# Expert matmuls of a mixture-of-experts layer in row tiles of 64, with destinations in rings of twelve

## What is computed

```python
C = CAP_FACTOR * ((A + E - 1) // E)          # 384 places for an expert
buf = zeros(E, C, D).at[se, pos_c].add(x[st])
g = jnp.einsum('ecd,efd->ecf', buf, w_gate)  # E 64, D 256, F 176
u = jnp.einsum('ecd,efd->ecf', buf, w_up)
eo = jnp.einsum('ecf,edf->ecd', jax.nn.silu(g) * u, w_down)
gathered = eo[se, pos_c] * (sw * valid)[:, None]
y = zeros_like(x).at[st].add(gathered)
```

## Time and profile before

| | before |
|---|---|
| median of 3 runs | 639.82 us |
| lowest, highest | 635.39, 646.47 us |
| span of the profiled execution | 538.8 us |
| TensorE busy, matmuls | 509.7 us, 95% |
| TensorE busy, weight loads | 425.6 us, 79% |
| VectorE, ScalarE, GpSimd busy | 345.0, 299.8, 334.1 us |
| DMA, mean | 221 GB/s |
| mean granted TensorE clock | 0.979 |

### The profile page before, as it was taken

One profiled execution on the slowest core, in us unless ns is written; L12 is line 12 of the kernel. 1 busy time (PEld: TensorE's weight loads), 2 busy tenths in 40 slices (PEclk: granted clock), 3 DMA queues, 4 the chain that ended last, 5 costly groups with the idle time before them and its releaser, 6 DMA issues.

```text
span 538.8 us, 13623 instructions
## 1 busy us (share of the span) xinstructions
PE 509.7 (95%) x4267; PEld 425.6 (79%) x4267; DVE 345.0 (64%) x1107; ACT 299.8 (56%) x899; POOL 334.1 (62%) x365
## 2 busy tenths in 40 slices
PE   8799999999999988998999999999999999999992
PEld 7698999889888877886777887777777877877681
DVE  3976888999999977753555555555554545456412
ACT  4797978999999842120444444545445444544420
POOL 4564254776566668730466776767777767778850
PEclk9898999999999979998999999999999999999997
DMA  8999999752222222269999999999999999967557
GB/s 283 402 375 395 401 400 385 233 212 102 94 92 102 103 75 100 105 211 317 234 256 235 240 235 239 245 241 247 267 236 249 236 241 245 241 110 118 58 121 155
DMA packets 65857, 119.01 MB, mean 221 GB/s; under 512 B 11216, under 2 KB 43280, under 8 KB 62704
## 3 DMA queue, kind: packets, MB, share of 16 engines
q0 software_dynamic: 24576, 56.39, 40.2%
q1 hardware_dynamic: 39584, 58.75, 35.4%
q10 hardware_dynamic: 1616, 2.90, 1.5%
HBM read 57.28 MB, written 60.23 MB: 218 GB/s over the span
## 4 chain that ended last, share of the span: by engine, by line
PE 55%; issue 1%; DMA 1%; DVE 1%; SPq 1%; ACT 0%; DVEq 0%
PE PS L960 18%; PE PS L978 10%; PE PS L964 8%; PE PS L981 7%; PE PS L947 4%; PE PS L811 3%; PE PS L797 2%; PE PS L786 1%; DMA XG<-expert_rows 1%; SPq L483 0%; SPq L470 0%; SPq L469 0%; SPq L468 0%; ACT YE L1236 0%; DVE hot L1410 0%
## 5 line engine op out<-in xcount | busy, mean ns | idle before, releaser
L1838 POOL DMA_INDIRECT expert_rows<-XR,slot x96 | 95.9, 999 | 50.7 <-issue 31.0
L1861 POOL DMA_INDIRECT acc_b<-YE,dest x64 | 93.7, 1465 | 43.9 <-issue 20.5
L1861 POOL DMA_INDIRECT out<-YE,dest x64 | 93.6, 1462 | 34.2 <-issue 13.3
L1236 ACT ACTIVATE YE<-PS,wsel 104x256 f32<-104x256 f32 (+14 forms) x128 | 53.5, 468 | 96.0 <-PE PS L981 96.0
L1063 ACT ACTIVATE SMX<-SMX,smax 128x112 f32<-128x112 f32 x256 | 75.0, 387 | 3.5 <-DVE smax L1466 3.5
L1651 DVE TENSOR_TENSOR HE<-SL,PS 128x216 f32<-128x216 f32 (+12 forms) x64 | 23.2, 362 | 56.1 <-ACT SL L1223 55.4
L1642 DVE COPY XET<-PS 128x432 f32<-128x432 f32 (+12 forms) x64 | 36.6, 572 | 18.8 <-PE PS L947 18.4
L1628 DVE SCALAR_TENSOR_TENSOR hit<-XG,by_rank 112x12 f32<-112x12 f32 (+3 forms) x64 | 14.6, 228 | 41.3 <-DMA acc_b<-YE,dest 21.9
L1223 ACT ACTIVATE SL<-PS 128x216 f32<-128x216 f32 (+12 forms) x64 | 21.6, 337 | 31.6 <-PE PS L960 30.8
L960 PE MATMUL PS<-XET,W 128*128 128x256 f32 (+9 forms) x192 | 38.3, 342 | 0.3 <-issue 0.2
L960 PEld LDWEIGHTS PS<-XET,W 128*128 128x128 f32 x192 | 30.8, 189 | 8.9 <-issue 8.2
(11 more groups left out here) (236 smaller groups left out, 1119.8 us busy)
## 6 DMA issues: line engine op xcount, KB each, us to landing
expert_rows<-zero POOLq DMA_DIRECT2D x24, 1088.0 KB, 13.8
W<-in_w SPq DMA_DIRECT2D x24, 368.0 KB, 3.8
XG<-expert_rows SPq DMA_DIRECT2D x24, 238.0 KB
XB<-in_w SPq DMA_DIRECT2D x15, 368.0 KB, 3.6
SMX<-in_w SPq DMA_DIRECT2D x15, 368.0 KB, 3.5
XG<-expert_rows SPq DMA_DIRECT2D x24, 204.0 KB
W<-in_w SPq DMA_DIRECT2D x24, 128.0 KB, 3.8
XG<-expert_rows SPq DMA_DIRECT2D x10, 272.0 KB
```

Of the source, the lines that this page charges most:

```text
L1236: act.mul(YE[0:h, e.slot, t, :], PS[0:h, 5 + t, e.odd * D:(e.odd + 1) * D], wsel[0:h, e.slot, t:t + 1]).then_inc(y_ready, 1)
L1838: pool.indirect_dma_start(rows, bass.IndirectOffsetOnAxis(ap=slot[:, d2 % UN, k:k + 1], axis=0), XR[:, d2 % UN, :], None, bounds_check=EX ...
L1861: pool.indirect_dma_start(target, bass.IndirectOffsetOnAxis(ap=dest[0:h, e.slot, t:t + 1], axis=0), YE[0:h, e.slot, t, :], None, bounds_ch ...
```

## The change

TensorE's part of the expert stage is written anew (the rare branch keeps the old form in `third_tiles`). Every product is cut into halves of 64 rows of the summed dimension, and a half on rows 0 to 63 is issued beside one on rows 64 to 127 that belongs to another result in another PSUM bank: gate beside up, tail beside gate, token tile beside token tile. Since two halves of one result meet in one bank, TensorE waits for its own earlier half (`h_half`, `d_half`). The down products run one step later, `down(e-1)` in step e, in two pieces. The rows are transposed 64 by 64, into two banks of which there is one pair instead of two, so a transpose waits for the copy of the expert just before. VectorE copies in two instructions, and does copy, choices, product, tail in this order; ScalarE weights `e-1` between the two silus. `dest` and `wsel` are rings of twelve, so `choices` waits for additions twelve experts back. SyncE's text is the same.

```diff
-        wsel = sb("wsel", [P, UN, 2])
+        wsel = sb("wsel", [P, AHEAD, 2])
-        dest = sb("dest", [P, UN, 2], I32)
+        dest = sb("dest", [P, AHEAD, 2], I32)
+        T_ps = PS[:, 0:2, 0:4 * HP].rearrange("p k (d t r) -> p k d t r", d=DC, t=2)
...
+                def waits_rows(e):
+                    hold(pe, xg_loaded[e.slot], e.turn(16, 16))
+                    if not e.first():
+                        hold(pe, et_evac, e.times(1))
+
+                def rows_t(e, t):
+                    for d in range(DC):
+                        for k in range(2):
+                            r = row_half(k)
+                            mm = pe.transpose(T_ps[:, k, d, t, :], XG[r, e.slot, t, d * P:(d + 1) * P], ident[r, r])
+                    return mm
+
+                def product(e, k, o, d, start=False, stop=False):
+
+                    q, n, r = e.odd, 2 * half(e), row_half(k)
+                    into = (PS[:, 2, 0:n], PS[:, UP[q], 0:n], PS[0:W1C - 2 * P, 3, 0:n])[o]
+                    return pe.matmul(into, W1S[home(e)][r, d, o * P:min((o + 1) * P, W1C)], XET[r, q, d, 0:n],
+                                     start=start, stop=stop)
+
+                def hidden_1(e):
+                    pe.wait_ge(ew_loaded[home(e)], e.turn(48, 48, AHEAD))
+                    pe.wait_ge(et_evac, e.times(1, 1))
+                    if not e.first():
+                        pe.wait_ge(silu_ready, e.times(2, -1))
+                    if not e.first(2):
+                        pe.wait_ge(h_ready, e.times(2, -3))
+                    product(e, 0, 1, 0, start=True)
+                    product(e, 1, 0, 0, start=True)
+                    product(e, 0, 1, 1)
+                    product(e, 1, 0, 1).then_inc(h_half, 1)
+
+                def hidden_2(e):
+
+                    pe.wait_ge(h_half, e.times(2, 1))
+                    if not e.first():
+                        pe.wait_ge(h_ready, e.times(2))
+                    product(e, 0, 0, 0)
+                    product(e, 1, 2, 0, start=True)
+                    product(e, 0, 0, 1, stop=True).then_inc(gu_done, 1)
+                    product(e, 1, 2, 1).then_inc(h_half, 1)
+
+                def hidden_3(e):
+
+                    pe.wait_ge(h_half, e.times(2, 2))
+                    product(e, 0, 2, 0)
+                    product(e, 1, 1, 0)
+                    product(e, 0, 2, 1, stop=True)
+                    product(e, 1, 1, 1, stop=True).then_inc(gt_done, 1)
...
+                def down_1(e):
+                    pe.wait_ge(h_ready, e.times(2, 2))
+                    pe.wait_ge(w2_doubled, e.times(1, 1))
+                    if not e.first():
+                        pe.wait_ge(y_ready, e.times(2))
+                    weighing(e, 0, 0, 0, start=True)
+                    weighing(e, 1, 1, 0, start=True)
+                    weighing(e, 0, 0, 1)
+                    weighing(e, 1, 1, 1).then_inc(d_half, 1)
+
+                def down_2(e):
+
+                    pe.wait_ge(d_half, e.times(1, 1))
+                    weighing(e, 0, 1, 0, stop=True)
+                    weighing(e, 1, 0, 0, stop=True).then_inc(dn_done, 1)
+
+                def step(e):
+                    nxt, ahead, last = e + 1, e + 2, e - 1
+                    if has(nxt, EX):
+                        hidden_1(nxt)
+                    if has(ahead, EX):
+                        waits_rows(ahead)
+                        rows_t(ahead, 0)
+                    if has(last, EX):
+                        down_1(last)
+                    if has(ahead, EX):
+                        rows_t(ahead, 1).then_inc(et_done, 1)
+                    if has(nxt, EX):
+                        hidden_2(nxt)
+                    if has(last, EX):
+                        down_2(last)
+                    if has(nxt, EX):
+                        hidden_3(nxt)
...
                 def step(e):
                     if has(e + 1, end):
-                        silus(e + 1)
+                        silu_main(e + 1)
+                    if has(e - 1, end):
+                        weighted(e - 1)
+                    if has(e + 1, end):
+                        silu_tail(e + 1)
+                    if has(e + 2, end):
+                        doubled(e + 2)
...
-                    if not e.first(UN):
+                    if nt == 1:
                         dve.wait_ge(y_stored[j], adds_before(e, nt))
+                    elif not e.first(AHEAD):
+                        dve.wait_ge(y_stored[j], e.turn(32, 32 - 32 * AHEAD // UN))
...
+                    if nt == 2:
+                        to = XET[:, e.odd, :, 0:n].rearrange("p d (t n) -> p d t n", t=2)
+                        dve.tensor_copy(to[:, :, :, 0:HP], T_ps[:, 0])
+                        dve.tensor_copy(to[:, :, :, HP:n // 2], T_ps[:, 1, :, :, 0:n // 2 - HP]).then_inc(et_evac, 1)
+                        return
```

More of the change, by code:

```diff
@@ L32 @@
 P = 128
+HP = P // 2
 T, D = 2048, 256
@@ L316, in build @@
         gu_done, gt_done = sem("gu_done"), sem("gt_done")
+        h_half, d_half = sem("h_half"), sem("d_half")
         silu_ready, h_ready = sem("silu_ready"), sem("h_ready")
@@ L939, in rows_t, with third_tiles @@
+            def third_tiles():
+                pe.wait_ge(et_evac, EX)
+                pe.wait_ge(y_ready, 2 * EX)
                 def rows_t(e):
-                    h = half(e)
                     pe.wait_ge(xg_loaded[e.slot], e.turn(16, 16))
[L943 to L948, removed]
+                    pe.wait_ge(et_evac, e.times(1, -1))
+                    for d in range(DC):
+                        mm = pe.transpose(PS[:, e.odd, d * MAIN:d * MAIN + P], XG[:, e.slot, 0, d * P:(d + 1) * P], ident[:, :])
@@ L968, in down @@
                 def down(e):
-                    j, q, h = home(e), e.odd, half(e)
+                    j, q = home(e), e.odd
                     pe.wait_ge(h_ready, e.times(2, 2))
[L972 to L975, removed]
+                    pe.wait_ge(y_ready, e.times(1, EX))
                     c = slice(q * D, (q + 1) * D)
[L977 to L983, removed]
+                    pe.matmul(PS[:, 5, c], HE[:, q, 0, 0:P], W2S[j][:, 0, :], start=True, stop=False)
+                    pe.matmul(PS[:, 5, c], HE[0:FT, q, 1, 0:P], W2S[j][0:FT, 1, :], start=False, stop=True).then_inc(dn_done, 1)
                 def step(e):
-                    if has(e + 1, end):
+                    if has(e + 1, 2 * EX):
                         hidden(e + 1)
-                    if has(e + 2, end):
+                    if has(e + 2, 2 * EX):
                         rows_t(e + 2)
                     down(e)
[L992 to L1004, removed]
-                in_flight(pe, step, half is even_half)
+                rows_t(Step(EX))
+                rows_t(Step(EX + 1))
+                hidden(Step(EX))
+                rest_in_flight(pe, step)
             def closing():
@@ L1246, in step, with third @@
                     if has(e + 1, end):
-                        silus(e + 1)
+                        silu_main(e + 1)
[5 more added lines that the diff above has]
+                        doubled(e + 2)
+                def third(e):
+                    if has(e + 1, end):
+                        silu_main(e + 1)
+                        silu_tail(e + 1)
                     weighted(e)
-                    if nt == 2 and has(e + 2, end):
-                        doubled(e + 2)
                 if nt == 1:
-                    silus(Step(EX))
-                    rest_in_flight(act, step)
+                    silu_main(Step(EX))
+                    silu_tail(Step(EX))
+                    rest_in_flight(act, third)
                     return
@@ L1257, in experts @@
                 doubled(Step(1))
-                silus(Step(0))
+                silu_main(Step(0))
+                silu_tail(Step(0))
                 in_flight(act, step, half is even_half)
+                step(Step(EX))
             def closing():
@@ L1659, in tail_products, with third @@
                         i = dve.tensor_tensor(HE[64 * t:64 * t + FT, q, 1, c], SL[0:FT, q, 1, c],
-                                              PS[64:64 + FT, TAIL[q], c], ALU.mult)
+                                              PS[64:64 + FT, 3 if nt == 2 else TAIL[q], c], ALU.mult)
                     i.then_inc(h_ready, 1)
                 def step(e):
+                    if has(e + 2, end):
+                        rows_t(e + 2)
+                    if has(e + 1, end):
+                        choices(e + 1)
+                        product(e + 1)
+                        tail_products(e + 1)
+                def third(e):
                     if has(e + 1, end):
@@ L1674, in experts @@
                 rows_t(first + 1)
-                if nt == 2:
-                    pair_add(NPAIR - 2)
-                    pair_add(NPAIR - 1)
+                if nt == 1:
+                    choices(first)
+                    product(first)
+                    tail_products(first)
```

(4 more changed lines are left out.)

76 lines of the change are left out of this document (50 added, 26 removed).

## The result

The changed kernel takes **681.5 us** in the median (677.7 to 691.3, 4 runs) where the kernel before takes 640.6 in the runs beside it: ratio 1.0625, 95% interval 1.057 to 1.068, or +40.8 us. The forecast was 677 us and +37.

The account below looks back on a forecast made before the run. TensorE was taken to bound the expert stage; after the change, late expert rows would. +40.6 for 52 steps, -2 at the start, -1.4 at the end sum to +37: 677 us, +5.8%, range 646 to 703.

Parts of the forecast that it names:

- The loop: Steps 3 to 55: late down products delay expert rows and stall transposes; 4.83 us a step for 4.05, +40.6 us; chance 0.77.
- SyncE's part: In SyncE's queue: from the down products' end, past three weight pieces, to the issue of the rows, 2.97 us.
- The landing: Expert rows, from issue to arrival behind the weights: taken as 4.1 us, range 2.9 to 5.1.
- Hardly depending on the rows: Steps 3 to 55: the stalled step stays about 4.83 us whatever number of rows the experts have.
- Steps 0 to 3 and the end: First steps lack a down product and save 0.4 each: -2 us; one more down and weighting at the end: +1.6.
- Steps 55 to 63: No weights left to fetch, so the loop is open: 3.56 us a step at GpSimd's pace for 3.94, -3.0 us.
- TensorE's own step: Expert stage at halves of 108 rows, nothing late: 3.82 us against 4.25, 0.43 saved.
- the sign of loads that bound: Starts of L962 in one row tile over 0.19 us apart at 216 columns would mean loads bound, not rows.
- a floor: GpSimd's issue of two additions for an expert: 3.46 us a step at small experts, under the 3.73 taken now.
- rows in time: Faster rival: expert rows arrive before their transposes, so no stall; -23 us, 617 us; chance 0.08.
- additions as a bound: Rival: additions bound anyway, so the change does nothing measurable; counted with the within-2% rival, chance 0.10.
- 101 us outside of the span: Median run of 639.8 us is 101 more than the profiled span; that distance was kept for the forecast.

Follow-up runs that it names:

- after_again: The changed kernel unchanged, run again on another chip: 684.11 us, ratio 1.065 to the kernel before.
- rows_early: The changed kernel with SyncE issuing expert rows first and weights one turn later: 547.05 us, ratio 1.002 to the kernel before on that chip.
- old_again: The kernel before, unchanged, run again for a second profile: 543.39 us, a single run.
- early_three: The row-tiled kernel with rows issued before weights, plus a third accumulator for additions and a second fold: 632.39 us, ratio 0.990 to the kernel before.

## Why the prediction was right, and where it was not

**The loop.** Right, and by its own terms. Forecast 4.83 us a step for steps 3 to 55, measured 4.86 and 4.83 (`after_again`); SyncE's part 2.97, measured 2.99. The landing was taken as 4.1 us; the 26 links of the chain hold 101.3 us, and without the first, slow one it is 3.8 each. From 370 to 612 us the chain makes 23 turns from one load of rows to the next. Sixteen of them take two steps at a granted clock of 1.00: 9.25 us in the median, or 4.6 a step, with 2.56 for TensorE (forecast 2.55) and 3.4 for the landing. In three the clock fell (below), and TensorE's part is 3.3 to 3.8 us; eight hidden instructions at 442.31 take 1.74 us that take 0.93 at 447.78. And four turns are three steps long, 13.4 to 16.2 us: the chain goes twice through SyncE's issues in them (about 7 us) or through more of TensorE's work. The prediction knew neither kind, and its landing was too long: that the mean comes to 4.83 is in part luck. "Hardly depending on the rows" held roughly: the first, second and last third of these steps are 5.24, 4.57 and 4.82 us in the first profile, 4.94, 4.76 and 4.78 in the second. Undoing SyncE's order removed the loss, and making it alone made 28 of 41 us, so the mechanism is shown by its removal and by its addition.

**Steps 0 to 3 and the end.** Forecast -2 and +1.6, measured -2.0 and +1.0 by the starts of the hidden products. From silu to silu it looks like 0 and +0.2: the first such step grew from 2.59 to 3.63 us, the next two fell from 4.72 to 4.16 and 4.24, and since the silus and the down products don't follow each other as before, the down products that are missing at the start and added at the end fall out of both parts. **Steps 55 to 63.** Forecast -3.0 (for 8 steps, while its 27.55 us are 7), measured -2.7 for 7 and -3.4 for 8. The sum in the span from the first silu is +38.5 in the first profile and +37.2 in the second, against +37. The other 2 us of the medians' +40.8 lie ahead of the first silu or between runs; that was not settled.

**TensorE's own step.** Right: 3.82 us at 108 rows when nothing is late, worked out as 3.82 (in `rows_early`; the whole 0.43 is measured, its division over passages and transposes isn't). Loads of two tiles do run side by side: two starts of L962 in one row tile are 0.183 us apart at 216 columns, in the median of `rows_early` and of the changed kernel, under the 0.19 that was named as the sign of loads that bound. The Trainium skill's rule that a load costs by its columns whatever its rows ("TensorE: Matmul & The Clock Gate", section "LDWEIGHTS (loading the stationary operand)"), weighed in the prediction, agrees with the trace for one load: 128 columns take 0.140 us with 84 rows and with 108 (L947) and 0.139 with 64 (L955). Two on different row tiles overlap here.

**Wrong: the additions.** The step that failed is the one that priced them at GpSimd's issue, "a floor" of 3.46 us an expert, and left out their landing. The profile of before had it: additions landed after 5.1 us in the median, and an expert's wait for those of e-2. With 1.73 us to the second issue, 5.0 to 5.4 to its landing and some 0.8 from there to the next issue, two experts take 7.6 to 8 us: 3.8 to 4.0 each. In `old_again` and in `rows_early` the additions of 39 of 62 experts start within 1.1 us of that landing; in the changed kernel, where rows are late, those of one do. The experiments that keep the order of e-2 and the full load, and have rows in time, lie at 3.99 to 4.05 us (4.10 with rings of four), whatever TensorE does; the one with a third array lies at 3.78. So the kernel before had two bounds within a tenth of a microsecond, TensorE at 4.06 and the additions at about 4.0, and the rival "rows in time" at 617 us could not have come true: with rows in time the kernel is at 1.00, not 0.96. The prediction named additions as a bound among the rivals, then set it aside because "two thirds of the steps are TensorE's". The trace had the better sign: `hit` waited for both targets, 40 us in all, and the prediction cited the 21.9 of one.

**Wrong: 101 us outside of the span.** A run's time is 2 us more than its span (679.4 and 677.6). The page of before came from an execution with a span of 538.8 us, and the runs of 635 to 646 us are like those of the chips on which the part ahead of the experts takes some 90 longer. The constant did no harm, because the change doesn't touch that part, but it was no launch cost.

**Sizes missed on the way.** Rings of twelve, 4 to 8 us forecast in the kernel before: nothing. Loading 296 of 544 KB of weights: 8 us of the 23 expected. A longer ring of outputs: slower by a few us.

## What to carry to other kernels

When an engine that issues transfers waits in order, a counter that comes later delays all that is issued behind the wait, not only what it guards: move or reorder work on the producer only after walking each counter that it raises to the last instruction queued behind it. And before you price a gain on the busiest engine, work out the period of every dependence that returns to itself (here: issue, landing, next issue to the same array), from landings in the trace and not from issue times; the second bound may stand a per cent behind the first.

## What the runs showed of the hardware

**The granted clock fell after some of TensorE's waits.** In the changed kernel it is 1.00 in most stretches of the stage, but after the idle 2.02 us ahead of 441.11 it fell. Stretches of 4 us (us, busy time of the engines, clock, DMA share, GB/s):

```profile
438.00:442.00 4.00, 1.98 (x24) 1.52 (x24) 0.92 (x3) 1.16 (x4) 2.65 (x2) 1.00 0.92 205
442.00:446.00 4.00, 4.00 (x30) 3.56 (x28) 1.29 (x6) 1.19 (x3) 0.29 (x1) 0.57 0.63 140
446.00:450.00 4.00, 4.00 (x52) 3.71 (x50) 2.16 (x10) 1.74 (x5) 2.95 (x2) 1.00 0.79 193
```

0.57 is the lower of its two levels (1.2 of 2.4 GHz) for most of a stretch, with 30 instructions for 52 in the next. There are three such falls from 400 to 475 us, where the clock averages 0.93 to 0.94, so they cost an estimated 5 us at most; from 475 to 625 us there is none, with waits of the same kind, and `after_again` has two in its whole stage. Why these waits and not the others no run shows.

**Additions into memory land late under load.** It takes 5.1 us in the median for some 100 KB in the kernel before, and 3.3 at the end of the stage when no weights are loaded, as in the last link of the chain of `early_three`, 3.32. The Trainium skill ("DMA: Bandwidth & Descriptors", section "Anatomy of one DMA — SWDGE (gpsimd) path") puts a transfer on GpSimd's path at about 2.0 us and its bytes at 436 GB/s, which would be an estimated 2.2 us for 100 KB; the measurement is over twice that, with the queues at a share of about 1.0 and the transfer adding to memory. Which of the two lengthens it more no run here settles, but shorter additions and fewer loads each took a microsecond off (4.0 and 4.2 for 5.0 to 5.4).
